# Last attention of a four-layer transformer kernel: VectorE gets an order of work of its own

## What is computed

```
def _qdq(x):
    s = jnp.maximum(jnp.max(jnp.abs(x), axis=-1, keepdims=True) / 127.0, 1e-08)
    return jnp.clip(jnp.round(x / s), -127.0, 127.0) * s
q = _qdq(x) @ _qdq(wq).T + bq
kv = cond @ wkv.T + bkv
k, v = jnp.split(kv, 2, axis=-1)
attn = jax.nn.softmax(jnp.einsum('bnhd,bmhd->bhnm', q, k) * scale, axis=-1)
o = jnp.einsum('bhnm,bmhd->bnhd', attn, v).reshape(B, N, C)
out = _qdq(o) @ _qdq(wp).T + bp
x = x + out            # called with _layernorm(x)
```

## Time and profile before

| | us |
|---|---|
| median of 3 runs | 2132.37 (2131.95 to 2136.18) |
| profiled execution, own time | 2131.96 |
| its span, first to last instruction | 2130.1 |
| PE busy | 2030.8 |
| VectorE busy | 1153.6 |
| ScalarE busy | 825.6 |
| last attention, its first scores to its last update (in the span) | 1703.8 to 1924.5 |

### The profile page before, as it was taken

The page is one execution under the profiler, slowest core; times in us unless marked ns, Lnnn a source line. Parts: engine busy times, 40 slices in busy tenths (PEclk is TensorE's granted clock), DMA queues, the critical chain, the costliest instruction groups (busy, mean ns, idle before and its releaser), DMA issues.

```text
span 2130.1 us, 28642 instructions
## 1 busy us (share of the span) xinstructions
PE 2030.8 (95%) x10556; PEld 1152.7 (54%) x10556; DVE 1153.6 (54%) x2597; ACT 825.6 (39%) x1717; POOL 182.1 (9%) x466
## 2 busy tenths in 40 slices
PE   8999999999999998999999999999899898888999
PEld 3444445444666444555555555566544455557665
DVE  1324455258122585666666666678666578863221
ACT  1333223312111364545544554455422255543331
POOL 1011110000000121111111111011100000000000
PEclk9999999999999999999999999999999989988999
DMA  6355442551642321020100001230001322210000
GB/s 235 137 217 203 160 170 105 195 217 45 210 150 75 148 104 43 23 102 23 30 22 23 22 22 44 73 100 23 20 16 54 116 88 83 81 56 6 11 11 15
DMA packets 60315, 185.12 MB, mean 87 GB/s; under 512 B 10578, under 2 KB 29010, under 8 KB 54463
## 3 DMA queue, kind: packets, MB, share of 16 engines
q1 hardware_dynamic: 58451, 145.55, 19.9%
q0 software_dynamic: 1728, 37.75, 4.6%
HBM read 124.61 MB, written 49.50 MB: 82 GB/s over the span
## 4 chain that ended last, share of the span: by engine, by line
PE 82%; DVE 11%; DMA 2%; issue 2%; ACT 2%; SPq 1%; POOL 0%; DVEq 0%; ACTq 0%
PE psum L120 57%; PE psum L113 8%; PE psum L1595 5%; PE psum L2677 5%; PE psum L1639 5%; DVE small L2556 2%; PE psum L1164 1%; PE psum L2485 1%; DVE R L1337 1%; DMA d_kv<-WK 1%; DVE R L1336 1%; DVE WK L2562 1%; DMA R<-in_wkv 1%; DVE WK L324 1%; DVE small L301 0%
## 5 line engine op out<-in xcount | busy, mean ns | idle before, releaser
L120 PE MATMUL psum<-R,WK 128*125 128x512 f32 (+10 forms) x3094 | 1043.5, 484 | 25.3 <-DMA WK<-in_ctxT 7.5
L120 PEld LDWEIGHTS psum<-R,WK 128*112 128x112 f32 (+4 forms) x3094 | 502.5, 170 | 514.5 <-issue 396.7
L113 PE MATMUL psum<-small,WK 112*125 112x112 f32 (+5 forms) x2036 | 278.8, 267 | 47.8 <-DVE WK L2562 11.3
L113 PEld LDWEIGHTS psum<-small,WK 112*125 112x125 f32 (+5 forms) x2036 | 224.7, 155 | 153.0 <-issue 86.9
L120 PE MATMUL psum<-WK,R 128*32 128x128 f32 (+3 forms) x1752 | 201.2, 358 | 4.3 <-ACT WK L2516 1.9
L120 PE MATMUL psum<-R 128*128 128x112 f32 (+4 forms) x832 | 146.4, 326 | 12.4 <-DVE R L1956 10.8
L120 PEld LDWEIGHTS psum<-WK,R 128*32 128x32 f32 (+3 forms) x1752 | 109.6, 137 | 68.5 <-issue 20.7
L120 PEld LDWEIGHTS psum<-R 128*128 128x128 f32 (+2 forms) x832 | 101.7, 180 | 58.2 <-issue 40.6
L1689 ACT ACTIVATE WK<-psum,small 112x487 f32<-112x487 f32 x128 | 96.9, 757 | 76.8 <-DVE small L1774 72.8
L1595 PE MATMUL psum<-R,WK 128*112 128x512 f32 x256 | 120.1, 592 | 0.0
L1771 DVE TENSOR_TENSOR psum<-psum,R 112x112 f32<-112x112 f32 x128 | 35.2, 275 | 150.9 <-PE psum L120 150.9
(11 more groups left out here) (239 smaller groups left out, 2157.7 us busy)
## 6 DMA issues: line engine op xcount, KB each, us to landing
R<-in_wf POOLq DMA_DIRECT2D x6, 4096.0 KB, 13.7
d_w<-R POOLq DMA_DIRECT2D x6, 2048.0 KB, 19.3
R<-d_w SPq DMA_DIRECT2D x6, 2048.0 KB, 10.8
WK<-in_ctxT SPq DMA_DIRECT2D x16, 750.0 KB, 6.5
d_v<-WK SPq DMA_DIRECT2D x16, 750.0 KB
R<-in_wq SPq DMA_DIRECT2D x7, 1024.0 KB, 8.2
R<-in_wo SPq DMA_DIRECT2D x6, 1024.0 KB, 16.0
d_k<-X SPq DMA_DIRECT2D x8, 750.0 KB, 4.8
```

The source lines that it names most:

```text
L113: ins = pe.transpose(dst, src, idn[0:k, 0:k])
L120: ins = pe.matmul(dst, lhs, rhs, start=k == 0, stop=k == len(pairs) - 1)
```

## The change

VectorE gets a list of its own, `dve_steps`, in place of `steps`. In it the normalization stands with p = 0, xi with p = 1, the statistics of the next batch (a kind of its own) and the addition of the output bias bp to x (likewise) with p = 2, ot with p = 3, oi with p = 4, q with p = 5 and y with p = 7. The rounding instruction (times reciprocal, plus MAGIC) moves from `scale_of` into `whole_numbers`. The addition of the bias is no longer a link of the chain. In `steps`, which PE, ScalarE and the order of the banks go by, the kinds norm, xi and oi, on which these engines did nothing, are gone, and xiT stands with p = 2, behind the o of that step, in place of p = 3.

```diff
-            steps, act_steps = [], []
+            steps, act_steps, dve_steps = [], [], []
...
-                rest += {1: [("norm", 0, 0)], 2: [("xi", 0, 0)], 3: [("ot", 0, 2), ("xiT", 0, 0), ("oi", 0, 2)],
-                         4: [("q", 0, 0)], 5: [("oiT", 0, 2)], 6: [("qT", 0, 0), ("y", 0, 2)]}.get(p, [])
+                rest += {2: [("xiT", 0, 0)], 3: [("ot", 0, 2)], 4: [("q", 0, 0)], 5: [("oiT", 0, 2)],
+                         6: [("qT", 0, 0), ("y", 0, 2)]}.get(p, [])
                 steps += [scores, turned] + rest
                 act_steps += [turned, scores] + rest
+                dve_steps += [scores, turned]
+                dve_steps += {0: [("norm", 0, 0)], 1: [("xi", 0, 0)], 2: [("stats", 0, 0), ("bias", 0, 2)], 3: [("ot", 0, 2)],
+                              4: [("oi", 0, 2)], 5: [("q", 0, 0)], 7: [("y", 0, 2)]}.get(p, [])
...
                 link(dve.reciprocal(rr, c))
-                link(dve.tensor_scalar(v, v, rr, MAGIC, ALU.mult, ALU.add))
...
             def whole_numbers(dve, b, name, v, vi):
+                dve_chain.on(dve)(dve.tensor_scalar(v, v, rr, MAGIC, ALU.mult, ALU.add))
...
-                    for kind, j, lag in steps:
+                    for kind, j, lag in dve_steps:
...
-                        elif kind == "xi":
-                            if b:
-                                whole_numbers(dve, b, "xi", xn, xi)
-                            if b + 1 < NB:
-                                ln_stats(dve, link, n, b + 1)
+                        elif kind == "xi" and b:
+                            whole_numbers(dve, b, "xi", xn, xi)
+                        elif kind == "stats" and b + 1 < NB:
+                            ln_stats(dve, link, n, b + 1)
+                        elif kind == "bias":
+                            dve.tensor_tensor(xr[:, b, :], xr[:, b, :], bp, ALU.add)
                         elif kind == "y":
...
-                            link(dve.tensor_tensor(xr[:, b, :], xr[:, b, :], bp, ALU.add))
```

## The result

The changed kernel's median is 2130.1 us (20 executions) against 2132.42 (20) before; the ratio is 0.9974, with a 95% interval of 0.9963 to 0.9986. That is a gain of a quarter of a per cent where 0.6% was forecast.

| executions of the changed kernel | number |
|---|---|
| 2119.3 to 2120.8 us | 7 |
| 2126.5 to 2136.7 us | 15 |
| 2151.5 to 2156.9 us | 9 |
| 5428.8 us | 1 |

A forecast was written before the change was run, and what follows sets the result against it. PE was taken as the bound, losing 3.2 us per batch to VectorE's lateness in the last attention. Gains 7.2 + 1.2 + 1.1 + 1.5 + 1.9 + 0.35 - 0.3 = 12.9 us took 2132.37 to 2119.5; range 2114 to 2127.

The forecast's parts named there:

- the clock rival: Last attention, iteration 1: q's 0.7 us move keeps PE at 1.2 GHz until the next q; 17.5 us, 2137, chance 9%.
- VectorE's lateness: Last attention: VectorE's late maximum and copy cause PE's stalls in four of eight slots (steps) per iteration, 3.2 us per batch.
- the relation: If VectorE's maximum is late by L, PE stalls in the next slot by L + 1.83 us minus slot length.
- Slot 2's new stall: PE in slot 2 of each full batch: 0.77 us newly lost to VectorE's lateness.
- slot 3's: PE's turn of pT(1)'s odd half waits for ScalarE's copy of xiT: 0.92 us lost; slot lost 1.19 before.
- slots 5 and 6: PE's stalls there, 0.2 and 1.06 us before, fall to none and about nothing (0.04).
- the gain per batch: New stalls of 1.7 us against 3.2 before: 1.45 us per full batch, 7.2 over five.
- y's wait: VectorE's 2.48 us wait for y in slot 7 disappears, and with it PE's 0.74 us stall in slot 0.
- the end of the stage: Iteration 8: s(7) to oT's copy shrinks from 10.3 to about 6.9 us, by 1.5 of idle and 1.9 of clock.
- The sum of 12.9 us: Total gain forecast over the last attention's full batches, its first and last iterations, and its end.
- The range: Kernel time of 2114 to 2127 us, meant to hold 8 in 10, reaching to the bounds of xiT's wait.
- the third rival: VectorE's order merely moves the stall, 3.2 us per batch remains, only the tail is gained: 2129, chance 5%.

The follow-up runs named there:

- e4: Changed kernel with xiT back in slot 3 for PE, ScalarE and the banks, VectorE's new order kept; 2113.9 to 2119.8 us, ratio 0.9931.
- e1: The changed kernel, unaltered, run again 12 times; 2119.5 to 2156.9 us in three groups, ratio 0.9974.
- e5: Changed kernel plus three products of 512 columns behind s(3) of iterations 3 to 8; six executions at 2121.3 to 2124.3 us, six at 2137.4 to 2140.1.
- e9: As e4, plus one wait making PE pause behind pT(0) of iteration 1; five executions at 2114.6 to 2117.3 us, seven at 2134.0 to 2138.1.
- e6: As e5, plus eight products in iteration 1's first pause, behind s(1); 2115.7 to 2128.1 us.
- e11: As e6, but with slot 3's added products from iteration 2 on; 2115.4 to 2118.5 us, ratio 0.9925.
- e3: Kernel before the change plus eight products behind s(1) of iteration 1; median 2129.6 us, ratio 0.9994.
- e7: Changed kernel with only xiT's move and what it needs; VectorE's ot, oi, q, bias and y in their former slots; median 2138.6 us, ratio 1.0020.

## Why the prediction was wrong

Two steps failed, both on PE's clock. The one that places the median is a term put at nothing: the stalls were priced by their length, and a fall of the clock behind them in mid-stage was not counted. The other is the reason given against the clock rival.

- **VectorE's lateness and the relation**: right. Slot 2's new stall was put at 0.77 (0.69 of idle and a slower restart measured), slot 3's at 0.92 (0.80 of idle and a restart), slots 5 and 6 at nothing. The waits of e4 were worked out beforehand by the same relation and came as 0.30 and 0.24. The period came to 24.29 us where the sum gave 24.1: the gain per batch is 1.23, not 1.45, since a block of pT that is released in two halves takes up to 0.1 us longer (1.00 against 0.91 in slot 6, and again in slot 3), and since ot and xiT, done apart, take 0.88 us (1782.83 to 1783.41 and 1779.15 to 1779.45) where together they took 0.77. Over five batches that is 1.1 us.
- **y's wait, the end of the stage**: right. 6.77 us where 6.9 was said.
- **The sum of 12.9 us**: right to 0.6 us for an execution without the later falls, in part because two errors cancel. In e1's profile, with the 10.2 us of its one fall in mid-stage taken out, s(2) of iteration 1 to s(7) of iteration 8 gives 8.6 us (195.13 before, 196.74 there) where 9.2 was forecast, and from that s(7) to the end of the span 4.9 us (228.2 and 223.3) where 3.75 was. The 7 of 32 executions at 2119.3 to 2120.8 lie where this sum puts them.
- **The clock rival**: its mechanism and its price were right (17.5 us forecast; 16 between the groups of e5, 18 in e9). It stood at 9% as what the kernel would do, and 9 of 32 executions do it; its time of 2137 is not the result, since those executions had later falls on top. The step that failed is "against: q is the same and nothing else in those slots changes". The rows had shown that the clock came back as one product ended; a thing with that little room had no claim to stay when that product moved by 0.6 us. Also its end was put wrongly: the clock came back in iteration 2's slot 3, a little ahead of the next q (s at 1759.12 has 0.89).
- **The drops in mid-stage**: missing altogether, and the reason why the median is 2130 and not 2119.5 (e1's profile, of 2130.41, has one of them, 20.5 us long and worth 10). The prediction counted each stall by its length and did not ask what it does to the clock. It used the clock for the one idle of 1.49 us at the stage's end and took the rest as full because the rows of before had 1.00 in all five batches. In the new order the stalls of slots 2 and 3 lie together, 0.69 and 0.80 us with 4 us from one restart to the next, where before the nearest two of over 0.6 us in different slots were 6.5 us apart (1799.91 and 1806.41). A pair does not always do it: 3 of 5 in the changed kernel's first profile, 1 of 5 in e1's. Shown: filling the second one takes the middle group away (e5, e6, e11), and moving it does (e4). Not shown: which spacing or length is still harmless; e3's and e7's drops have other pairs.
- **The range** of 2114 to 2127 would have had to hold the median of a distribution with three groups, and it was made for one with a single peak. That 2130.1 lies close to the third rival's 2129 is chance: its mechanism, 3.2 us per batch remaining, is not what happened (the period is 24.29, not 25.5).

## What to carry to other kernels

A list of slots with the lateness of the slower engine, carried from slot to slot, gave the stalls of the changed kernel and of e4 to within 0.15 us (e7's period came out 0.8 us shorter than expected) and a better order than the one tried; put the big pieces where the other engine has room, and ask of each shared bank whose copy stands behind whose exponentials. Then read the granted clock beside every pause, including those that a change will make: if the clock returns at one certain product, treat the place of that product as a thing that the change can break. And look at all executions, not at a median: here 2119, 2130 and 2153 were one program.

## What the runs showed of the hardware

- TensorE can stay at 1.2 GHz with no gap in its work that the profile shows: 31 us in the changed kernel's profile (1726.5 to 1757.5), within a stretch of 51.2. The Trainium skill (TensorE: Matmul & The Clock Gate, Part 1) says that activity releases the throttle; here the trace does not agree, since PE was busy and the clock stayed down. Why it came back at q in some executions and in iteration 2's slot 3 in others (there at 1759.0, during ot) is left open beyond what the nine profiles above show.
- Where the clock came back: of the 25 returns between the first scores and s(7) of iteration 8 in the 14 profiles, 22 lie in a bf16 product of 512 columns (q, y or the eight products) or up to 0.6 us behind it. Not every such product brings it back: e1's drop of 20.5 us passes a whole q (1845.33, 1.96 us long).
- It can drop from 2.4 to 1.2 GHz in a stretch in which PE is 94% busy (22.5 of 24 us between 1782 and 1806), with no pause over 0.81 us.
- A shift of 0.6 us in one product moved 7 of 12 executions by 18 us. That it is seven of twelve and not all or none means that something that differs from execution to execution takes part; the profiles point to the moment of the clock's fall at the stage's start (0 to 0.6 us behind the first scores). Drops in earlier stages, whose code is the same, also differ between executions: the stage's first scores came at 1703.8, 1705.8 and 1707.7 us in three profiles.
